# One attention and mixture-of-experts kernel: low-rank rows stored as one block, GpSimd's list reordered, the first attention steps moved

## What is computed

```
xn = layernorm(x)
q, k, v = (xn @ basis.T) @ (amp * cos(phase)).T        # each through 32 "harmonics": low rank
attn = softmax(q k^T / 4) v, 16 heads of 16;  then the same low-rank form for the output
moe: 8 experts (256 -> 352 -> 256), the 2 best of each token, weighted
shared: (silu(xn @ sw_gate) * (xn @ sw_up)) @ sw_down  # 256 -> 704 -> 256
out = x + attn + moe + shared
```

## Time and profile before

| What | Value |
|---|---|
| Median of 3 timed runs | 995.96 us (995.03 to 998.99) |
| The profiled execution's own time | 991.98 us |
| Its span, first to last instruction | 990.2 us |
| PE / DVE / ACT / POOL busy | 89% / 62% / 59% / 41% |
| Mean granted TensorE clock | 0.95 |

### The profile page before, as it was taken

The page is one execution under the profiler, slowest core; times in us unless marked ns, Lnnn a source line. Parts: engine busy times, 40 slices in busy tenths (PEclk is TensorE's granted clock), DMA queues, the critical chain, the costliest instruction groups (busy, mean ns, idle before and its releaser), DMA issues.

```text
span 990.2 us, 19557 instructions
## 1 busy us (share of the span) xinstructions
PE 882.8 (89%) x6491; PEld 616.1 (62%) x6492; DVE 613.8 (62%) x923; ACT 580.6 (59%) x935; POOL 407.1 (41%) x411
## 2 busy tenths in 40 slices
PE   4745999999999986999999998989989999989996
PEld 3435999999999974555464464555455555446452
DVE  7867834434443454776776775766766686776762
ACT  4746644444444433757757756756756766766764
POOL 2003522222222233825825815733833752752831
PEclk9965999999999998999999999989999999999999
DMA  9983655222222126464565655554655664644411
GB/s 314 382 253 136 209 144 168 74 73 70 69 74 70 47 91 148 143 166 129 171 173 134 185 153 131 163 154 121 182 153 128 175 167 117 184 125 99 107 31 43
DMA packets 89928, 140.04 MB, mean 141 GB/s; under 512 B 17304, under 2 KB 51616, under 8 KB 87936
## 3 DMA queue, kind: packets, MB, share of 16 engines
q1 hardware_dynamic: 83168, 121.24, 42.4%
q0 software_dynamic: 6480, 17.70, 6.7%
q10 hardware_dynamic: 208, 0.14, 0.0%
HBM read 79.24 MB, written 54.71 MB: 135 GB/s over the span
## 4 chain that ended last, share of the span: by engine, by line
PE 59%; DMA 18%; DVE 7%; POOL 5%; ACT 4%; issue 4%; SPq 3%; DVEq 0%; ACTq 0%; POOLq 0%
PE s_pair L1290 8%; PE bank L1308 8%; PE bank L1512 7%; PE bank L1449 6%; PE st_pair L1290 6%; PE s_pair L1363 4%; PE bank L1409 4%; DMA low_rank_rows<-ro 4%; PE st_pair L1437 4%; DMA r_rows<-low_rank_rows 3%; DMA o_sum<-inverse_rows 3%; DMA inverse_rows<-o_inv 2%; PE bank L1298 2%; DVE top L1867 2%; PE bank L1273 2%
## 5 line engine op out<-in xcount | busy, mean ns | idle before, releaser
L1867 DVE TENSOR_REDUCE top<-s_pair 128x2 f32<-128x1024 f32 x248 | 303.8, 1225 | 166.6 <-PE s_pair L1363 159.0
L1082 ACT ACTIVATE prob<-st_pair 128x1024 f32<-128x1024 f32 x252 | 258.3, 1025 | 109.4 <-PE st_pair L1437 105.6
L755 POOL DMA_INDIRECT xg<-xn_rows,token_of x71 | 78.5, 1106 | 216.7 <-PE bank L1273 161.9
L1409 PE MATMUL bank<-xT_b,w_sh 64*128 64x512 f32 x960 | 146.5, 411 | 0.4
L1363 PE MATMUL s_pair<-k_rows,q_rows 48*128 48x512 f32 x496 | 117.8, 469 | 13.1 <-DVE top L1867 10.8
L1437 PE MATMUL st_pair<-q_rows,k_rows 50*128 50x512 f32 x504 | 109.2, 428 | 19.7 <-ACT prob L1082 11.0
L1449 PE MATMUL bank<-prob,v_ones 128*32 128x512 f32 x1024 | 126.5, 613 | 0.0
L1409 PEld LDWEIGHTS bank<-xT_b,w_sh 64*128 64x128 f32 x960 | 93.6, 191 | 30.7 <-issue 8.4
L793 POOL TENSOR_TENSOR ao<-ao,o_sum 128x512 f32<-128x512 f32 x15 | 19.3, 1287 | 183.6 <-DMA o_sum<-inverse_rows 183.6
L1308 PE MATMUL bank<-w_exp,c_hT 128*128 (+1 forms) x639 | 94.2, 292 | 0.3 <-ACT c_y L994 0.3
L777 POOL TENSOR_TENSOR h_f<-h_f,u_half 128x512 f32<-128x512 f32 x40 | 51.6, 1291 | 92.3 <-DVE h_f L1882 92.0
(11 more groups left out here) (230 smaller groups left out, 1249.9 us busy)
## 6 DMA issues: line engine op xcount, KB each, us to landing
qk_rows<-qk_hi SPq DMA_DIRECT2D x56, 256.0 KB
q_rows<-qk_rows SPq DMA_DIRECT2D x64, 192.0 KB
k_rows<-qk_rows SPq DMA_DIRECT2D x56, 192.0 KB
expert_rows<-c_y SPq DMA_DIRECT2D x71, 128.0 KB, 1.7
xn_T_split<-x_T SPq DMA_DIRECT2D x8, 1024.0 KB, 6.6
xT_b<-xn_T_split SPq DMA_DIRECT2D x7, 1024.0 KB, 8.6
qk_rows<-qk_lo SPq DMA_DIRECT2D x28, 256.0 KB
x_all<-in_L_attn_x_dram SPq DMA_DIRECT2D x8, 512.0 KB, 8.1
```

The lines of the kernel that those rows point to most:

```text
L755: pool.indirect_dma_start(xg[s % 4][:, :], None, xn_dram, bass.IndirectOffsetOnAxis(token_of[:, s:s + 1], 0)).then_inc(c_x[s % 4], 16)
L1082: act.activation(prob[n % 3][:, 2 * jp:2 * jp + 2, :].rearrange("p j l -> p (j l)"), score_T_pair(b, g, t)[:, :], ACT.Exp, scale=HD ** -0. ...
L1409: ins = pe.matmul((g_bank, u_bank)[up][:, :], w_sh[rows, a, o:o + P], xT_of(b)[rows, c, k, :], start=(n == 0 and i == 0), stop=(n == 1 and ...
L1867: dve.tensor_reduce(top[g % 2][:, :, jp, qt], score_pair(b, g, v)[:, :].rearrange("p (i k) -> p i k", i=2), AX_X, ALU.max).then_inc(d_max, 1)
```

## The change

Four things are changed.

1. The DRAM buffer of the low-rank rows is (2, 96, 512) instead of (2, 32, 3, 512). The stores write 96 rows in order; the load back rearranges.
2. GpSimd's list: `sum_y` stands ahead of the `hidden_low` that it followed; the copies stand later, and `sum_y(b, 2)` stands behind `hidden(b, 4)` and `ao_low`.
3. `q_rows` and `k_rows` of group 1 move to another place in memory, and `load_rows(0, 1)` is issued at tile 66, while tiles still run. In `slot_first` the maxima come first and `load_rows(0, 2)` stands ahead of `load_low_rank(1)`.
4. `slot(-1, 3)` is gone; each engine has its work written out behind the tiles. On PE the turned maxima and the first score stand ahead of `low_rank(1)`, and the gate/up pieces and scores follow in a closer order.

```diff
-    r_dram = nc.dram_tensor("low_rank_rows", (2, 32, 3, L), F32).ap()
+    r_dram = nc.dram_tensor("low_rank_rows", (2, 96, L), F32).ap()
...
+        q_rows1 = sb("q_rows1", [P, 2, L], F32R, late)
+        k_rows1 = sb("k_rows1", [P, 2, L], F32R, late)
...
         def slots(slot):
 
-            slot(-1, 3)
...
-            sp.dma_start(r_dram[LO].rearrange("h n l -> n h l"), e_lo[0][0:96, :].bitcast(F32)).then_inc(r_st, 16)
+            sp.dma_start(r_dram[LO], e_lo[0][0:96, :].bitcast(F32)).then_inc(r_st, 16)
...
                 if s == 66:
                     load_xT(1)
+                    load_rows(0, 1)
...
-                    sp.dma_start(r_rows[b % 2][c * HARM:(c + 1) * HARM, :, :].bitcast(F32), r_dram[part]).then_inc(r_in, 16)
+                    sp.dma_start(r_rows[b % 2][c * HARM:(c + 1) * HARM, :, :].bitcast(F32), r_dram[part].rearrange("(n h) l -> h n l", n=3)).then_inc(r_in, 16)
...
             def slot_first():
-                load_rows(0, 1)
+                load_max(0, 0)
                 store_low_rank(1)
-                load_max(0, 0)
+                load_rows(0, 2)
                 load_low_rank(1)
-                load_rows(0, 2)
...
                 if there(b + 1):
+                    gather_at(b + 1, 1, 3, 6) if there(b) else gather_y(0, 1)
                     hidden_low(b + 1, 0)
-                    gather_at(b + 1, 1, 3, 6) if there(b) else gather_y(0, 1)
...
                 gather_at(b, 2, 0, 1)
+                sum_y(b, 0)
                 hidden_low(b, 1)
-                sum_y(b, 0)
                 gather_at(b, 3, 0, 3)
                 hidden(b, 2)
                 gather_at(b, 4, 0, 5)
+                sum_y(b, 1)
                 hidden_low(b, 2)
-                sum_y(b, 1)
                 gather_at(b, 5, 0, 7)
                 hidden(b, 3)
                 gather_at(b, 6, 1, 1)
-                hidden_low(b, 3)
                 if there(b - 1):
                     normalise(b - 1, 1)
-                sum_y(b, 2)
                 gather_at(b, 7, 1, 3)
+                hidden_low(b, 3)
                 hidden(b, 4)
                 if there(b - 1):
                     ao_low(b - 1, 1)
+                sum_y(b, 2)
                 hidden_low(b, 4)
                 sum_y(b, 3)
...
# ACT
+            max_rows(0, 0)
             low_rank_high(1)
-            max_rows(0, 0)
+            tanh(0, 0)
+            up_half(0, 0)
+            values_out(0, 0)
+            hidden_high(0, 0)
             slots(slot)
...
# PE
-                    low_rank(1)
                     down(NS - 1, END - 1, at[run + 1])
-                    turn_max(0, 0)
...
+            turn_max(0, 0)
+            score(0, 1, 0)
+            low_rank(1)
             pe.wait_ge(c_yk, NS)
             pe.wait_ge(c_hed, NS)
+            for n in range(3):
+                gate_up_shared(0, 0, n)
+            score(0, 1, 1)
+            gate_up_shared(0, 0, 3)
+            score(0, 1, 2)
+            project_values(0, 0)
+            score(0, 1, 3)
+            for n in range(4):
+                gate_up_shared(0, 1, n)
...
# DVE
             split_max(0, 0)
+            maximum(0, 1, 0)
             low_rank_low(1)
+            maximum(0, 1, 1)
             dve.wait_ge(c_yk, NS)
             dve.memset(v_ones[:, :, :, HD:2 * HD], 1.0).then_inc(ones_ok, 1)
+            maximum(0, 1, 2)
+            gate_shared(0, 0)
+            maximum(0, 1, 3)
```

More of the change, by code:

```diff
@@ L229, in build_program @@
         qk_lo = [sb(f"qk_lo{i}", [P, L], F32R, late) for i in range(2)]
-        q_rows = [None] + [sb(f"q_rows{g}", [P, 2, L], F32R, late) for g in range(1, NG)]
-        k_rows = [None] + [sb(f"k_rows{g}", [P, 2, L], F32R, late) for g in range(1, NG)]
+        q_rows = [None, q_rows1] + [sb(f"q_rows{g}", [P, 2, L], F32R, late) for g in range(2, NG)]
+        k_rows = [None, k_rows1] + [sb(f"k_rows{g}", [P, 2, L], F32R, late) for g in range(2, NG)]
         u_half = sb("u_half", [P, L], F32, late)
@@ L503, in _ @@
             load_first_rows(1, e_hi)
-            sp.dma_start(r_dram[HI].rearrange("h n l -> n h l"), e_hi[0][0:96, :].bitcast(F32)).then_inc(r_st, 16)
+            sp.dma_start(r_dram[HI], e_hi[0][0:96, :].bitcast(F32)).then_inc(r_st, 16)
             sp.wait_ge(d_r, 1)
             load_first_rows(2, e_lo)
-            sp.dma_start(r_dram[LO].rearrange("h n l -> n h l"), e_lo[0][0:96, :].bitcast(F32)).then_inc(r_st, 16)
+            sp.dma_start(r_dram[LO], e_lo[0][0:96, :].bitcast(F32)).then_inc(r_st, 16)
             for e in range(1, EARLY):
@@ L561, in load_first_values @@
                 for c, part in enumerate((HI, HI, LO)):
-                    sp.dma_start(r_rows[0][c * HARM:(c + 1) * HARM, 2, :].bitcast(F32), r_dram[part, :, 2, :]).then_inc(r_in, 16)
+                    sp.dma_start(r_rows[0][c * HARM:(c + 1) * HARM, 2, :].bitcast(F32), r_dram[part, 2 * HARM:3 * HARM, :]).then_inc(r_in, 16)
             def store_y(s, i):
@@ L606, in store_low_rank @@
                 wait(sp, a_r, b + 1)
-                sp.dma_start(r_dram[HI].rearrange("h n l -> n h l"), r_hi[:, :].bitcast(F32)).then_inc(r_st, 16)
+                sp.dma_start(r_dram[HI], r_hi[:, :].bitcast(F32)).then_inc(r_st, 16)
                 wait(sp, d_r, b + 1)
-                sp.dma_start(r_dram[LO].rearrange("h n l -> n h l"), r_lo[:, :].bitcast(F32)).then_inc(r_st, 16)
+                sp.dma_start(r_dram[LO], r_lo[:, :].bitcast(F32)).then_inc(r_st, 16)
             def load_low_rank(b):
@@ L1114, in slot @@
                         up_half(c, q)
-                    if t == 5 and there(nb) and now:
+                    if t == 5 and there(nb):
                         max_rows(nb, ng)
@@ L1127, in slot @@
                         ao_high(ppb, ppg // 2)
-                    if t % 4 == 1 and what == "pair":
+                    if t % 4 == 3 and what == "pair":
                         hidden_high(c, q)
@@ L1133, in slot @@
                         qk_high(b + 1, PROJECTED.index((g, t)))
-                    if g == 3 and t == 2 and there(b + 2) and now:
+                    if g == 3 and t == 2 and there(b + 2):
                         low_rank_high(b + 2)
@@ L1369, in turn_max @@
                 more = there(b + 1)
-                if g == 0:
+                if (b, g) == (0, 0):
+                    pe.wait_ge(c_hed, NS - 1)
+                elif g == 0:
                     wait(pe, d_r, b + 2) if more else wait(pe, d_po, (b - 1) * 2)
@@ L1456, in low_rank @@
                 wait(pe, xT_in, b * 16)
-                if b == 2:
-                    wait(pe, a_mt, 4)
+                if b <= 2:
+                    wait(pe, a_mt, 1 if b == 1 else 4)
                 else:
@@ L1471, in project_values @@
                     wait(pe, a_mt, b * NG + 1)
+                    if b == 0:
+                        pe.wait_ge(d_r, 2)
                 elif there(b + 1):
@@ L1568, in next_score @@
                 if t < STEPS - AHEAD:
-                    if there(nb) and there(b):
+                    if there(nb):
                         score(nb, ng, t + AHEAD)
@@ L1593, in small @@
                     project_o(b - 1, t // 4)
-                if g == 3 and t == 2 and there(b + 2) and there(b):
+                if g == 3 and t == 2 and there(b + 2):
                     low_rank(b + 2)
@@ L1614, in slot @@
                         values(b, g, 1)
-                    if t == 4 and there(nb) and now:
+                    if t == 4 and there(nb):
                         turn_max(nb, ng)
@@ L1939, in slot @@
                     if t < STEPS - AHEAD:
-                        if there(nb) and now:
+                        if there(nb):
                             maximum(nb, ng, t + AHEAD)
@@ L1943, in slot @@
                         maximum(qb, qg, t - STEPS + AHEAD)
-                    if t == STEPS - AHEAD - 1 and there(nb) and now:
+                    if t == STEPS - AHEAD - 1 and there(nb):
                         split_max(nb, ng)
@@ L1959, in slot @@
                         qk_low(b + 1, PROJECTED.index((g, t - 1)))
-                    if g == 3 and t == 3 and there(b + 2) and now:
+                    if g == 3 and t == 3 and there(b + 2):
                         low_rank_low(b + 2)
```

## The result

| | before | after |
|---|---|---|
| Median of timed runs | 995.5 us (4 runs, 993.9 to 999.0) | 956.95 us (4 runs, 955.0 to 959.6) |
| Ratio, 95% interval | 1 | 0.961 (0.957 to 0.965) |
| Profiled execution, its span | 991.98, 990.2 us | 955.04, 953.2 us |
| Mean granted TensorE clock | 0.95 | 0.968 |

The kernel is 3.9% faster. The predicted 962 (946 to 984) held it. One of its terms (what PE waits for `r_rows`) had the wrong size, and one (the price of GpSimd's new order) was taken off for nothing, since one edit was not costed at all. The two errors pulled in opposite directions, so the point came out closer than its terms were.

The account below looks back on a forecast made before the run. PE, busy 89% of the span, was taken as the bound, losing time only in stalls and at its lower clock. 1.5 + 16 + 5.5 + 8.6 - 8 + 10 = 33.6 us gave 962 us (946 to 984).

Parts of the forecast that it names:

- what PE waits for `r_rows`: Last slot of a batch: with short stores PE's waits for `r_rows` and `top_T` go, 16 of 17.6 us (10 to 17.6).
- the price of GpSimd's new order: GpSimd in each batch: sum 1 ahead of copy 2 makes hidden(3) late, -8 us (0 to -15).
- The stores: Low-rank stores to DRAM: 96 rows use 16 DMA engines instead of three, a pair costs 2 to 3 us instead of 7.9.
- My 1.5: Prologue: ACT's wait of 4.8 us for the low-rank store, half of 3.1 us taken back (0 to 3.1).
- The first steps: Behind the tiles: earlier loads and reordered work bring the first exponent to about 386 instead of 391.3, 5.5 us (3 to 7.5).
- GpSimd's order: GpSimd in each batch: sum 2 behind hidden(4) removes seven of PE's waits for exponents, 8.6 us (4.3 to 8.6).
- The clock: PE in the batches: the lower clock behind long stalls cost 13.0 us, of which 10 come back (4 to 13).
- Rival 1: Low-rank stores: DRAM is slow, not three engines, so the layout buys nothing; 11 us left, 985; chance 0.12.
- Rival 2: Batches: GpSimd becomes the bound, the wait moves from hidden(4) to hidden(3); 17.3 us left, 979; chance 0.13.
- rival 3: Batches: slower, two sums stand ahead of copies and the next product, rows land later; some 1015; chance 0.04.
- rival 4: Batches: gains cancel, as PE is held by DVE's maxima, one score at a time; about 994; chance 0.03.

Follow-up runs that it names:

- the three stores: The kernel after with the old DRAM layout, each low-rank store written as three stores of 32 rows: 957.71 us, ratio 0.9582.

## Why the prediction was right, and where not

**The stores: right, and why is shown.** A store of 192 KB lands in 2.1 us, and `top_T` gives back its 8.3 us whole. In the prologue the first gather of the kernel after starts at 85.90, 3.1 us earlier; with the layout alone it is 2.3. My 1.5 assumed that half would be lost; all of it, or nearly, arrives. It is no accident of one execution: the gather starts at 88.8 to 90.5 in the six kernels with the old stores, at 84.8 to 85.9 in the seven profiles with short ones and parts 3 and 4.

**`r_rows`: the failed size.** I took 16 of 17.6 us back, and 8.3 + 1.6 = 9.9 came, just under my low end of 10. The step that failed is "`r_rows` can be issued at 459.2, right behind the q load, 2.0 us earlier, and without the stores' backlog ahead of it". It was issued that much earlier (2.4 us). But there was no backlog of stores to lose: in the kernel before the load is issued only when the store has landed, and it takes 5.5 to 7.4 us all the same (chain of waits). What stands ahead of it, before and after, are the 768 KB of k and q rows. With the 576 KB of `r_rows` themselves they take an estimated 6.6 us at the 208 GB/s of the row at 449, and 7.14 to 7.64 us were measured. And PE, which no longer waits 1.2 us for `top_T`, arrives that much earlier. Putting the load first removed the wait; changing its pieces did not.

**The first steps: right.** 5.5 predicted, 5.3 measured by themselves; "about 386" was 385.98 and 386.33. In the kernel after, 7.65 us are gained up to the first exponent, 3.1 of them in the prologue:

```profile
383.66 1.02 ACT L1083 ACTIVATE prob<-st_pair 128x1024 f32<-128x1024 f32 x1
```

**GpSimd's order: right for unit 4, and for unit 3 right about the product and wrong about who waits.** The 8.6 us of exponent waits went. The price of 8 us rested on "the product is 1.6 us late [...] the 1.2 us to spare hide a part". The product is late, even by 2.5 us in the batch shown, but ACT's copy of it had been moved two steps back, and I had read over that edit. It hides the delay; with it undone some 4 to 7 us of my 8 appear. So this term was 0 instead of -8, for a reason that stands in the full change and not in the prediction. The list itself was also underpriced: with ACT's copy at step 3, the old list costs 24 to 27 us, by the clock and by a wait for `ao_T` that I had not looked for.

**The clock: right.** In the five stretches after, (1 - clock) x length sums to 1.4 us (0.02 x 72), against 13.0 before: 11.6 for my 10. Its one stretch at the lower clock, 529.9 to 533.3, comes right behind the longest wait that is left, 2.09 us for `r_rows` ahead of 528.87. More executions say the same: on one chip the mean clock of the whole span is 0.937 to 0.953 before and 0.951 to 0.966 after. It is not the gain of one part: between 430 and 930 us the mean clock is 0.97 before and with the layout alone, 0.98 with the list alone, 0.99 in the kernel after with the old layout, and 1.00 in the kernel after.

**The sum.** 3.1 + 9.9 + 4.5 + 8.6 + 0 + 11.6 = 37.7 us, less 1.5 that PE waits longer for DVE's maxima (12.3 against 10.8): 36.2, against 37.0 between the two spans. I had 33.6: two errors of about 6 and 8 us stood against each other, which is luck. Had only the first been put right, the forecast would have been 968, with only the second 954, both still in the range. Rival 1 is refuted by the three stores, and by the 22 us of the layout alone. Rival 2's mechanism, the late product of unit 3, is there but covered; its higher price, rival 3, did not come. Of rival 4 the 1.5 us are all that shows.

## What to carry to other kernels

Look at the outermost count of both sides of each DMA: 3 there made a 192 KB store take 7.9 us and what was queued behind it late, and either a layout of 96 rows or three stores of 32 repairs it. When a load is late, add up the bytes that stand ahead of it in the queue at the rate of the trace, and issue first what is needed first. When a product, its high copy and its remainder are on three engines, move the reader on one engine and the list on the other together: ACT's later copy alone made the kernel 0.5% slower, and was worth some 4 to 7 us beside the new list. And look into the whole change for edits that a summary of it leaves out: the one that was overlooked here had a price of its own.

## What was not expected of the hardware

The issue of the store on SP became shorter with the pattern, from 0.69 us to 0.30 for the same 192 KB; the three stores of 64 KB take 1.25 us of SP together. And executions of one kernel differ, for the most part along with the clock: on one chip the spans of the kernel before go from 993.9 us at a mean granted clock of 0.946 to 1003.5 at 0.933. The clock isn't all of it, as 997.5 and 1001.5 us both have 0.941. The profiled execution of before, 991.98 us, lies below all of those, so its rows may show less of the low clock than a usual execution has.
